# Top-32 pieces one step later, and the second expert layer's turning begun inside the attention's tail

## The chip, the cores and the metric

One core of a Trainium2 chip runs the whole kernel in one launch. The metric is the device time of an execution in microseconds; the time of a kernel is the median of its runs. Five engines work beside each other and meet through semaphores: TensorE (PE; PEld is its weight load), VectorE (DVE), ScalarE (ACT), GpSimd (POOL) and SyncE (SP), which issues most of the DMAs.

## The reference, cut to what matters

A decoder of two layers on `x` (2 x 512 tokens of 128) and a context (2 x 77 tokens of 128). Each layer adds three sublayers, each behind a layer norm. The second layer is where most of the change lies:

```python
# layer 1, behind layer 0 (attention, cross attention, experts that pick tokens)
x = x + L1_attn(layernorm(x))     # 16 heads of 64, causal softmax, then w_o
x = x + L1_xattn(layernorm(x))    # 16 heads of 8 on the 77 context tokens: scores, the 32
                                  # largest of a row, softmax over these, weighted values, Wo
x = x + L1_ffn(layernorm(x))      # 8 experts, the 2 best of a token:
#   h = relu(x @ Wg[e].T) * (x @ Wu[e].T); out_e = h @ Wd[e].T; sum of shares * out_e
```

## The kernel before

The tokens are worked in four blocks k of 256 (k = 0, 1 are batch 0, k = 2, 3 batch 1). The programs of the five engines are written out by hand, one loop for each engine over the same steps, and the order of each engine's instructions is the order of these loops.

**Attention of layer 1.** 48 steps U (`NU`), each one or two (head pair, query tile) units. At step U TensorE makes the scores of U + 2, turns the weights of U (`turn`, waiting for GpSimd's `divide(U)`) and sums values; VectorE finds row maxima (`row_max(U + 2)`) and reciprocal sums (`row_inv(U + 1)`), ScalarE copies the turned weights (`evac_pt(U)`) and makes the exponentials (`exps(U + 2)`), GpSimd divides (`divide(U + 1)`).

**Top-32 pieces.** The cross attention of layer 1 is cut into 16 pieces n of 4 heads x 256 tokens (4 pieces a block). A piece takes four quarters r on VectorE: in each eight MAX8 find the 8 largest of a row and eight MATCH_REPLACE8 remove them (`eight`, `remove`, lines 1207 and 1217). Around it: TensorE's `scores_x(n + 1)` and ScalarE's copy at r = 0, GpSimd's `shift(n)` at r = 1 and `gone(n - 1)`, `pick(n - 1)` (the mask and its product) at r = 0, ScalarE's exponential at r = 2, TensorE's transposes `weights_x(n - 1)` at r = 1 and 2 with ScalarE's copies `weights_T`, and `context(n - 1)` at r = 2. Pieces 0 to 9 run beside the attention, at steps that `piece_of(U)` names. Pieces 10 to 15 run behind it, at a late step `at` that `piece_late(at)` names (line 82): the helpers `cross`, `cross_one` and `cross_two` of each engine look it up.

**Late steps.** Three loops follow the attention, on every engine:
- b = 0 to 7, *the turning of the experts*. For each expert TensorE turns three 512-column parts of its weights (`turn_f(b, k)`, line 2473), ScalarE copies the first two as high parts (`w_hi`, line 1751) and the third as it is (`fd`), TensorE subtracts the high part (`minus_hi`), ScalarE copies the rest as low parts (`w_lo`, line 1755). Banks alternate over two experts. At b = 0 come route, the choice of two experts for batch 0's tokens and the last output projection; VectorE then works out the places of the tokens sorted by expert, GpSimd scatters the rows (line 800) and SP loads them back as 15 tiles of 128 sorted rows (`xs`, line 601). Before the steps b ≥ 2 end, `keep_busy` adds three matmuls without use (bank 7).
- j = 0 to 14 (`NS`), *the sorted tiles* of batch 0: `up_rows`, relu on ScalarE, `gate` on VectorE (line 1334), `hidden_T`, ScalarE's `evac_h`, `down_rows`. At j = 1, 5 and 9 `rows_T` turns the next four tiles into the same bank 7 that `hidden_T` uses.
- i = 0 to 31, *the dense half steps* of batch 1: all 8 experts for both blocks k = 2, 3, with `up`, `gate`, `down` and `combine`.

The late step is b, then 8 + j, then 23 + i. The norms, the context projection and the choice of experts for blocks 2 and 3 stand at fixed j and i behind the pieces that they need.

**What a wait for bank 4 means.** All late work of the top-32 pieces and of their norms goes through bank 4; `four` is the pair (semaphore, count) that says when ScalarE or VectorE has read what lies in it. In the same way `seven` guards bank 7.

```python
def piece_late(step):
    return divmod(40 + step, 4) if step <= 26 else (None, None)
```

Of the kernel before, what the change touches and what calls it, by code (L numbers as in the profile page):

```python
# [81 lines left out]
def piece_late(step):  # L82

    return divmod(40 + step, 4) if step <= 26 else (None, None)
# [26 lines left out]
def decoder(nc, x_in, ctx_in, a0_wq, a0_bq, a0_wk, a0_bk, a0_wv, a0_bv, x0_wq, x0_bq, x0_wk, x0_bk, x0_wv,  # L111
# [5 lines left out]
    with ExitStack() as held:  # L117
# [498 lines left out]
        def _(pool):  # L616
# [137 lines left out]
            for U in range(NU):  # L754
# [14 lines left out]
                if U + 1 < NU:  # L769
                    divide(U + 1)  # L770
# [58 lines left out]
            for j in range(NS):  # L829
                if j == 6:  # L830
                    rstd_two(2, gn_var, gn_rstd)
# [3 lines left out]
                if j == 9:  # L835
                    tokens_lo(2)
            for i in range(2 * E):
                if i == 7:
                    rstd_two(3, gn_var, gn_rstd)
                if i == 10:  # L840
# [7 lines left out]
        def _(dve):  # L848
# [401 lines left out]
            for U in range(NU):  # L1250
# [3 lines left out]
                if U + 1 < NU:  # L1254
# [160 lines left out]
            for j in range(NS):  # L1415
                gate(j)
                if j == 3:
                    context_norm(2)
                if j == 5:
                    add_context(2, ps[:, 4, 0:2 * P])  # L1420
                if j == 10:
                    gates(1, 4, 2, 4)
                if j == 12:
# [4 lines left out]
            for i in range(4 * E):  # L1428
# [3 lines left out]
                if i == 4:  # L1432
                    context_norm(3)
                if i == 6:
                    add_context(3, ps[:, 4, 0:2 * P])
                if i == 11:
                    gates(2, 6, 2, 4)
                if i == 13:
                    shares_of(2, 6, 2)
                if i == 14:  # L1440
# [8 lines left out]
        def _(act):  # L1449
# [232 lines left out]
            for U in range(NU):  # L1682
# [26 lines left out]
                evac_pt(U)  # L1709
                if U + 2 < NU:  # L1710
# [19 lines left out]
                if r == 1 and n >= 1:  # L1730
# [83 lines left out]
            for b in range(E):  # L1814
# [5 lines left out]
                cross_one(b)  # L1820
                for k in range(2):
# [8 lines left out]
                if b == 7:  # L1830
                    evac_xs(0)
            relu(0)
            for j in range(NS):
# [8 lines left out]
                if j == 3:  # L1842
                    evac_cn(2, four)
                if j == 6:
                    apply_two(2, gn_rstd, gn_ready)
                if j == 7:
                    norm_two(2, gnT_ps, gnT_ready, four)
                if j == 9:
                    tokens_hi(2)
                if j == 10:  # L1850
                    gates(1, 4, 2)
            for i in range(4 * E):
# [6 lines left out]
                if i == 4:  # L1859
                    evac_cn(3, four)  # L1860
                if i == 7:
                    apply_two(3, gn_rstd, gn_ready)
                if i == 8:
                    norm_two(3, gnT_ps, gnT_ready, four)
                if i == 9:
                    tokens_hi(3)
                if i == 11:
# [4 lines left out]
        def _(pe):  # L1872
# [158 lines left out]
            def values_x():  # L2031
                pe.wait_ge(qx_ready, 2)
                for b in range(B):
                    vo = ps[0:NC, 1, b * D:(b + 1) * D]
                    mm(vo, ctxT[:, b, :], w_x1T[:, 2, :], stop=False)
                    last = mm(vo, ones[0:1, 0:NC], bias_row("x1_bv"), start=False)
                last.then_inc(cross_ps, 1)
# [334 lines left out]

# [351 lines left out]
```

## Time and profile before

| | us |
|---|---|
| median of 3 runs | 583.12 |
| the runs | 580.05, 583.12, 586.41 |
| profiled execution | 580.95 |
| its span, first to last instruction | 579.2 |
| mean granted TensorE clock of it | 0.991 |

The span has these stages: layer 0 up to about 130 us, the attention of layer 1 up to 389.4, the turning of the experts up to 426.8, the sorted tiles up to 489.1, the dense half steps up to the end. Times in the rows below are microseconds from the span's start. A row of a timeline gives the start, the time from the first start to the last end, the engine, the line, the operation with what it writes and reads, and in brackets the idle time ahead of it with what ended it. Many instructions of TensorE have one line because one helper records them.

### The profile page before, as it was taken

Reading aid. Unit: us, or ns where it says so; the run is one execution under the profiler, and the core shown is the slowest. Engines: PE = TensorE matmul, PEld = TensorE weight load, DVE = VectorE, ACT = ScalarE, POOL = GpSimd, SP = SyncE. Lnnn points to the kernel's source line nnn. Section 1 sums busy time; section 2 is a strip of 40 time slices with the busy share of each in tenths; the row PEclk is TensorE's granted clock in tenths of the full one; section 3 lists DMA queues with packets and bytes.
Section 4 is the critical chain, followed back from the end, with each engine's and each line's share of the span. In section 5 each row is a group of like instructions: output and inputs, shape, how many; then the busy total and the mean of one; then the engine's idle time right before and its main releaser. Section 6 shows DMA issues by size and latency. Waiting matters only on the chain.

```text
span 579.2 us, 12144 instructions
## 1 busy us (share of the span) xinstructions
PE 515.3 (89%) x3947; PEld 409.7 (71%) x3947; DVE 385.4 (67%) x2194; ACT 311.1 (54%) x779; POOL 224.8 (39%) x236
## 2 busy tenths in 40 slices
PE   4888779998998999988999879978899899999997
PEld 2566348856667667767677657767767778999997
DVE  3576866543533697766598899968957979544533
ACT  2243324437785777665875667646765565323221
POOL 5014940013444474553564556552831343430000
PEclk9999999999999999998998999989999999999999
DMA  4700105604000000000000000004500000000000
GB/s 111 219 1 15 55 16 169 195 11 156 1 1 0 3 1 2 1 2 1 2 2 2 2 1 2 1 2 131 191 2 15 15 15 20 24 24 2 28 1 10
DMA packets 24089, 21.04 MB, mean 36 GB/s; under 512 B 2175, under 2 KB 18643, under 8 KB 24027
## 3 DMA queue, kind: packets, MB, share of 16 engines
q1 hardware_dynamic: 23515, 19.21, 11.0%
q0 software_dynamic: 512, 1.05, 0.6%
q8 instruction: 33, 0.54, 0.4%
q14 instruction: 29, 0.24, 0.1%
HBM read 17.22 MB, written 3.03 MB: 35 GB/s over the span
## 4 chain that ended last, share of the span: by engine, by line
PE 61%; DVE 15%; ACT 12%; issue 6%; POOL 5%; DMA 1%; DVEq 0%; ACTq 0%; POOLq 0%
PE ps L1874 51%; PE ps L2267 5%; ACT w_mem L1604 3%; DVE wk L1217 2%; PE ps L2329 2%; DVE sel_mem L1024 2%; ACT f_mem L1566 2%; DVE top L1207 1%; ACT pr L1604 1%; POOL xs_dram L800 1%; DVE nmax L1162 1%; PE ps L2541 1%; DVE bn L855 1%; POOL wk L743 1%; DVE xn L868 1%
## 5 line engine op out<-in xcount | busy, mean ns | idle before, releaser
L1162 DVE TENSOR_REDUCE nmax<-ps 128x2 f32<-128x256 f32 (+1 forms) x64 | 51.2, 821 | 59.6 <-PE ps L1874 57.5
L1217 DVE MATCH_REPLACE8 wk<-top,wk 128x77 f32<-128x77 f32 x384 | 80.6, 224 | 0.0
L712 POOL TENSOR_TENSOR w_mem<-w_mem,rinv 128x256 f32<-128x256 f32 (+3 forms) x44 | 53.1, 1218 | 50.9 <-DVE rinv L1168 50.4
L1334 DVE TENSOR_TENSOR sel_mem<-gr,ps 128x512 f32<-128x512 f32 x47 | 32.2, 686 | 48.3 <-ACT gr L1810 47.8
L1810 ACT ACTIVATE gr<-ps 128x512 f32<-128x512 f32 x47 | 28.1, 598 | 60.0 <-PE ps L1874 59.9
L1207 DVE MAX8 top<-wk 128x8 f32<-128x77 f32 x384 | 58.0, 224 | 0.2
L1874 PE MATMUL ps<-cat_mem 64*128 64x256 f32 (+7 forms) x276 | 56.8, 483 | 1.5 <-ACT cat_mem L1588 1.5
L1617 ACT ACTIVATE prT<-ps 128x768 f32<-128x768 f32 (+1 forms) x48 | 42.4, 883 | 21.3 <-PE ps L2267 20.8
L743 POOL TENSOR_SCALAR wk<-wk 128x616 f32<-128x616 f32 x16 | 28.1, 1754 | 53.7 <-DVEq L1221 53.4
L1604 ACT ACTIVATE w_mem<-ps,nmax 128x128 f32<-128x128 f32 (+3 forms) x88 | 44.5, 521 | 3.4 <-DVE nmax L1162 3.3
L1874 PE MATMUL ps<-prT,cat_mem 128*64 128x128 f32 x640 | 42.8, 281 | 3.3 <-DVE x L1242 1.8
L1874 PEld LDWEIGHTS ps<-prT,cat_mem 128*64 128x64 f32 x640 | 35.2, 139 | 9.6 <-issue 5.0
L712 POOL TENSOR_TENSOR pr<-pr,rinv 128x768 f32<-128x768 f32 (+3 forms) x20 | 26.6, 1341 | 28.0 <-DVE rinv L1168 27.6
L1874 PE MATMUL ps<-fd,sel_mem 128*128 128x128 f32 x256 | 34.5, 278 | 1.5 <-DVE sel_mem L1334 1.5
L1874 PE MATMUL ps<-x_hi,w_hi 128*128 128x256 f32 x128 | 34.6, 304 | 0.0
L1874 PEld LDWEIGHTS ps<-fd,sel_mem 128*128 128x128 f32 x256 | 31.2, 192 | 2.9 <-DVE sel_mem L1334 2.8
L1874 PE MATMUL ps<-later,ident 128*128 128x512 bf16 (+1 forms) x124 | 30.7, 369 | 1.8 <-ACT sel_mem L1665 0.7
L1874 PE MATMUL ps<-x_hi,w_lo 128*128 128x256 f32 x128 | 31.9, 282 | 0.0
L1588 ACT ACTIVATE cat_mem<-ps 128x512 f32<-128x512 f32 x32 | 19.4, 606 | 22.8 <-PE ps L1874 22.6
L2267 PE MATMUL ps<-ident,w_mem 128*128 128x128 f32 x212 | 30.5, 280 | 1.3 <-ACT cat_mem L1588 0.9
L1874 PEld LDWEIGHTS ps<-vh,sel_mem 77*128 77x128 f32 x256 | 29.8, 192 | 2.0 <-issue 0.9
L1217 DVE MATCH_VALUE_LOAD wk<-top,wk 128x8 f32 x384 | 30.9, 80 | 0.0
(362 smaller groups left out, 1313.9 us busy)
## 6 DMA issues: line engine op xcount, KB each, us to landing
w_mem<-in_L_ffn_W_dram SPq DMA_DIRECT2D x12, 256.0 KB, 3.2
f_mem<-in_L_ffn_Wg_dram SPq DMA_DIRECT2D x8, 256.0 KB, 2.9
f_mem<-in_L_ffn_Wu_dram SPq DMA_DIRECT2D x8, 256.0 KB, 3.7
f_mem<-in_L_ffn_Wd_dram SPq DMA_DIRECT2D x8, 256.0 KB, 4.2
sel_mem<-slot_dram SPq DMA_DIRECT2D x7, 256.0 KB
sel_mem<-in_L_ffn_W_dram SPq DMA_DIRECT2D x4, 256.0 KB, 4.0
xs_dram<-zero SPq DMA_DIRECT2D x1, 960.0 KB, 6.5
ys_dram<-f_mem SPq DMA_DIRECT2D x15, 64.0 KB, 1.5
```

Source lines behind the costliest of these rows:

```text
L712: pool.tensor_tensor(pr[s][:, :, at:at + n], pr[s][:, :, at:at + n], rinv[:, i % 8, :].unsqueeze(2).to_broadcast([P, 2, n]), ALU.mult)\
L743: pool.tensor_scalar(wk[q][:, :, :, :], wk[q][:, :, :, :], NEG, None, ALU.is_le)\
L1162: dve.tensor_reduce(nmax[:, i % 8, :], ps[:, 2 * s:2 * s + 2, at:at + (c + 1) * P], X, ALU.max, negate=True).then_inc(nmax_ready, 1)
L1207: dve.max(top[q][:, t, h, 8 * r:8 * r + 8], src[:, t, h, :]).then_inc(top_step, 1)
L1217: dve.match_replace(wk[q][:, t, h, :], top[q][:, t, h, 8 * r:8 * r + 8], src[:, t, h, :], GONE).then_inc(top_step, 1)
L1334: dve.tensor_tensor(hg[s][:, :], gr[s][:, :], ps[:, 2 * s + 1, :], ALU.mult)\
L1588: act.activation(qk_place(j), ps[:, bank, :].rearrange("p (w n) -> p w n", w=2), ACT.Copy)\
L1604: act.activation(pr[U % 3][:, h, at:at + (c + 1) * P], ps[:, 2 * s + h, at:at + (c + 1) * P], ACT.Exp, bias=nmax[:, i % 8, h:h + 1], accum ...
L1617: act.activation(prT[U % 3][:, :, 0:n], ps[:, 4:6, 0:n], ACT.Copy).then_inc(ptc_ready, 1)
L1810: act.activation(gr[j % 2][:, :], ps[:, 2 * (j % 2), :], ACT.Relu).then_inc(gr_ready, 1)
L1874: return pe.matmul(dst, lhsT, rhs, start=start, stop=stop, skip_group_check=shared)
L2267: last = pe.transpose(tiles(4 + h)[:, k, :], pr[U % 3][:, h, k * P:(k + 1) * P], ident[:, :])
```

## The change

- `piece_late` counts one step later: the late pieces begin at b = 1 instead of b = 0, and seven quarters instead of eight lie beside the turning. What followed a piece at a fixed j or i (context norm, its projection, norm, route and choice of block 2 and 3) moves by one step with it, but for the choice of block 2 at j = 14.
- Turning: two of the three parts of expert 0 (`turn_f(0, 0)`, `turn_f(0, 1)`, banks 0 and 1) move into step U = 45 of the attention. The three fillers of each b ≥ 2 go, the seven at the end become four and stand behind a wait for expert 6 only. The wait for the tile list and the loads of the first three tile numbers move from b = 1, 1, 2, 3 to b = 4, 4, 5, 6. At b = 7 `rows_T(0)` and ScalarE's `evac_xs(0)` stand ahead of the last corrections and low copies.
- Tail of the attention: ScalarE's first `weights_T(8)` stands ahead of the exponentials of U = 47; the reciprocals and the division of U = 47 stand ahead of `add_context(1)` and `rstd_two(1)`.
- Cross attention of layer 0: `values_x` is cut in two, and the halves stand ahead of and behind `weights_T0(1)`; the three fillers behind become six.

The diff, cut to its core:

```diff
 def piece_late(step):
-    return divmod(40 + step, 4) if step <= 26 else (None, None)
+    return divmod(39 + step, 4) if 1 <= step <= 27 else (None, None)
...
# GpSimd, attention
+                if U == NU - 2:
+                    divide(NU - 1)
                 for k in range(2):
                     if U == OUT[k] + 2:
                         rstd_two(k, gn_var, gn_rstd)
...
-                if U + 1 < NU:
+                if U + 1 < NU - 1:
                     divide(U + 1)
...
# VectorE, attention
-                if U + 1 < NU:
+                if U + 1 < NU - 1:
                     row_inv(U + 1)
...
+                if U == NU - 3:
+                    row_inv(NU - 1)
                 for k in range(2):
                     if U == OUT[k] + 1:
                         add_context(k, ps[:, 6, 0:2 * P])
...
# ScalarE, attention
                 evac_pt(U)
+                if U == NU - 3:
+                    weights_T(n - 1, 0, 7)
                 if U + 2 < NU:
                     exps(U + 2)
...
-                if r == 1 and n >= 1:
+                if r == 1 and n >= 1 and U != NU - 3:
                     weights_T(n - 1, 0, 7)
...
# ScalarE, turning
                 cross_one(b)
+                if b == 7:
+                    evac_xs(0)
                 for k in range(2):
                     evac_lo(b, k, F_BANKS[b % 2][k])
...
-                if b == 7:
-                    evac_xs(0)
...
# TensorE, layer 0
             context0(0)
+            values_x(0)
             weights_T0(1)
+            values_x(1)
             context0(1)
-            keep_busy(7, 3)
-            values_x()
+            keep_busy(7, 6)
...
# TensorE, attention (turn_f itself is only moved up)
                     if U == OUT[k] + 1:
                         project_context(k, six, (cat_ready, (26, 30)[k]))
+                        if U == NU - 3:
+                            turn_f(0, 0, (ex_ready, 2 * through(NU - 2)))
+                            turn_f(0, 1)
...
# TensorE, turning
+                    elif b == 0 and k < 2:
+                        continue
                     else:
                         turn_f(b, k)
...
-                if b >= 2:
-                    keep_busy(7, 3)
+                if b == 7:
+                    seven = rows_T(0, (place_step, 4))
                 for k in range(2):
                     minus_hi(b, k)
...
-                if b == 1:
+                if b == 4:
                     pe.wait_ge(place_step, 4)
-                if b in (1, 2, 3):
-                    experts.append(expert_of_tile(b - 1))
-                if b == 7:
-                    seven = rows_T(0, (place_step, 4))
+                if b in (4, 5, 6):
+                    experts.append(expert_of_tile(b - 4))
+            pe.wait_ge(w_lo_ready, 2 * E - 2)
+            keep_busy(0, 4)
             pe.wait_ge(fT_ready, 3 * E)
             pe.wait_ge(w_lo_ready, 2 * E)
-            keep_busy(0, 7)
             up_rows(0)
...
# sorted tiles and dense half steps, TensorE (as an example; the other engines likewise)
-                if j == 3:
+                if j == 4:
                     four = context_T(2, out_x, *four)
-                if j == 4:
+                if j == 5:
                     four = project_context(2, out_x, *four)
...
```

## Rows read from the trace of the kernel before

**Rows 1.** The page, its first line.
```profile
span 579.2 us, 12144 instructions
```

**Rows 2.** Four stretches: length, busy us of PE, PEld, DVE, ACT, POOL, PEclk, DMA.
```profile
372.00:389.40 17.40, 13.80 (x120) 11.07 (x121) 12.85 (x99) 8.34 (x18) 10.91 (x9) 0.90 0.01 2
389.40:426.80 37.40, 33.17 (x239) 27.76 (x239) 30.84 (x247) 27.44 (x58) 15.31 (x15) 1.00 0.41 126
426.80:489.10 62.30, 57.27 (x367) 47.66 (x368) 50.00 (x357) 33.41 (x74) 24.33 (x19) 1.00 0.05 14
489.10:579.20 90.10, 85.45 (x719) 83.50 (x717) 44.91 (x169) 25.57 (x49) 12.65 (x13) 1.00 0.05 15
```

**Rows 3.** The chain of waits, attention's tail: start, us, engine, what, line.
```profile
376.29 1.44 ACT pr L1604 x4
377.74 0.48 ACT sel_mem L1665
...
378.26 0.88 PE ps L2329 x4
```

**Rows 4.** Short stretches in the tail, columns as in rows 2.
```profile
376.50:377.00 0.50, 0.00 (x0) 0.00 (x0) 0.50 (x5) 0.50 (x3) 0.50 (x1) 1.00 0.04 16
...
380.00:381.00 1.00, 1.00 (x8) 0.67 (x9) 0.89 (x7) 0.55 (x1) 0.82 (x2) 0.50 0.00 0
```

**Rows 5.** Timeline of TensorE in the tail, the same matmuls twice.
```profile
368.94 1.75 PE L1874 MATMUL ps<-prT,cat_mem 128*64 128x128 f32 x28
...
380.35 2.53 PE L1874 MATMUL ps<-prT,cat_mem 128*64 128x128 f32 x28
```

**Rows 6.** Timeline of TensorE, turning and first sorted tile.
```profile
390.31 1.55 PE L2482 MATMUL ps<-ident,f_mem 128*128 128x128 f32 x12
...
401.68 1.54 PE L2482 MATMUL ps<-ident,f_mem 128*128 128x128 f32 x12 [1.86 <-issue]
...
412.48 0.81 PE L1874 MATMUL ps<-later,ident 128*128 128x512 bf16 x3
...
418.02 0.63 PE L2329 MATMUL ps<-ident,ex_mem 128*77 128x128 f32 x4 [0.93 <-POOL ex_mem L750]
...
426.84 1.67 PE L1874 MATMUL ps<-later,ident 128*128 128x512 bf16 x7 [0.60 <-ACT w_lo L1755]
...
428.16 0.58 PE L1874 MATMUL ps<-w_hi,xs_hi 128*128 x1
...
432.26 0.76 PE L1874 MATMUL ps<-kh,qc 128*128 128x308 f32 x2
```

**Rows 7.** Timeline of VectorE: last instruction of the tile list, two gates.
```profile
400.51 0.16 DVE L1368 TENSOR_SCALAR tile_id<-tile_e 1x15 int32<-1x15 f32 x1
...
430.66 0.69 DVE L1334 TENSOR_TENSOR sel_mem<-gr,ps 128x512 f32<-128x512 f32 x1 [5.91 <-ACT gr L1810]
...
434.05 0.68 DVE L1334 TENSOR_TENSOR sel_mem<-gr,ps 128x512 f32<-128x512 f32 x1
```

**Rows 8.** Timeline of ScalarE in the turning, high and low copies.
```profile
411.46 1.10 ACT L1751 ACTIVATE w_hi<-ps 128x512 fp32r<-128x512 f32 x2
...
413.68 1.08 ACT L1755 ACTIVATE w_lo<-ps 128x512 fp32r<-128x512 f32 x2
```

**Rows 9.** Timelines of GpSimd and SP: first row scatter, reloads of the sorted rows.
```profile
403.58 1.25 POOL L800 DMA_INDIRECT xs_dram<-xn,place_id  x1 [0.19 <-issue]
...
414.99 2.29 SPq L601 DMA_DIRECT2D xs<-xs_dram  x4
```

**Rows 10.** DMA issues, 380 to 440 us: count, KB each, median us to landing.
```profile
xs<-xs_dram SPq DMA_DIRECT2D x3, 256.0 KB, 4.0
```

**Rows 11.** TensorE's waits, 427 to 491 us: total us, times, longest us.
```profile
PE ps L2512 <- ACT f_mem L1772: 2.2, 3, 0.7
...
PE ps L1874 <- ACT sc L1644: 1.0, 2, 0.5
```

**Rows 12.** Timeline of TensorE in layer 0's cross attention.
```profile
46.62 0.66 PE L2048 MATMUL ps<-ident,cat_mem 128*77 128x128 f32 x4 [0.71 <-ACT cat_mem L1488]
```

More of the change, by code:

```diff
@@ L829, in _ @@
             for j in range(NS):
-                if j == 6:
+                if j == 7:
                     rstd_two(2, gn_var, gn_rstd)
@@ L1841, in _ @@
                 cross_two(E + j)
-                if j == 3:
+                if j == 4:
                     evac_cn(2, four)
-                if j == 6:
+                if j == 7:
                     apply_two(2, gn_rstd, gn_ready)
-                if j == 7:
+                if j == 8:
                     norm_two(2, gnT_ps, gnT_ready, four)
-                if j == 9:
+                if j == 10:
                     tokens_hi(2)
-                if j == 10:
+                if j == 11:
                     gates(1, 4, 2)
@@ L2029, in keys, with values_x @@
                 mm(ps[:, 0, 0:B * NC], w_x1T[:, 1, :], ctxT[:, :, :]).then_inc(cross_ps, 1)
-            def values_x():
+            def values_x(b):
                 pe.wait_ge(qx_ready, 2)
[L2033 to L2037, printed above, removed]
+                vo = ps[0:NC, 1, b * D:(b + 1) * D]
+                mm(vo, ctxT[:, b, :], w_x1T[:, 2, :], stop=False)
+                last = mm(vo, ones[0:1, 0:NC], bias_row("x1_bv"), start=False)
+                if b == B - 1:
+                    last.then_inc(cross_ps, 1)
             def scores_x0(b):
@@ L2371, in turn_two, with turn_f @@
                 return ((xnT_ready, 7 + k),)
+            def turn_f(m, k, *free):
+                for signal, count in free:
+                    pe.wait_ge(signal, count)
+                if k == 0:
+                    pe.wait_ge(in_f1[m % 4], 48 * (m // 4 + 1))
+                for c in range(FC):
+                    part_f = fn[m % 4][:, k, c, :]
+                    if k == 2:
+                        part_f = fn[m % 4][:, 2, :, :].rearrange("d a b -> d (a b)").rearrange("d (p c) -> d c p", c=FC)[:, c, :]
+                    last = pe.matmul(tiles(F_BANKS[m % 2][k])[:, c, :], part_f, ident[:, :], start=c == 0, stop=c == FC - 1,
+                                     is_transpose=True, skip_group_check=True)
+                last.then_inc(fT_ps, 1)
             pe.wait_ge(xin_ready, E)
@@ L2468, in _ @@
                         project_context(k, six, (cat_ready, (26, 30)[k]))
+                        if U == NU - 3:
+                            turn_f(0, 0, (ex_ready, 2 * through(NU - 2)))
+                            turn_f(0, 1)
                     if U == OUT[k] + 3:
                         norm_two(k, gn_ready, gnT_ps, gnT_ready, six, (v_ready, 15), (cat_ready, (27, 31)[k]))
-            def turn_f(m, k, *free):
-                for signal, count in free:
-                    pe.wait_ge(signal, count)
-                if k == 0:
-                    pe.wait_ge(in_f1[m % 4], 48 * (m // 4 + 1))
-                for c in range(FC):
-                    part_f = fn[m % 4][:, k, c, :]
-                    if k == 2:
-                        part_f = fn[m % 4][:, 2, :, :].rearrange("d a b -> d (a b)").rearrange("d (p c) -> d c p", c=FC)[:, c, :]
-                    last = pe.matmul(tiles(F_BANKS[m % 2][k])[:, c, :], part_f, ident[:, :], start=c == 0, stop=c == FC - 1,
-                                     is_transpose=True, skip_group_check=True)
-                last.then_inc(fT_ps, 1)
             def route(k, first, n, bank, *free):
```

46 lines of the change are left out of this document (23 added, 23 removed).

## The prediction

> **What bounds the kernel now.** I read the page first, then the stretches of the four stages that the change touches, then the chain of waits and the timelines of single engines inside them. The span is 579.2 us [rows 1], and 207 us of it lie in the stages from the attention's tail to the end [rows 2]. In none of the four is an engine full: TensorE is busy 13.8 of 17.4 us in the tail, 33.17 of 37.4 while the second expert layer's weights are turned, 57.27 of 62.3 over the 15 sorted row tiles (4.15 us a tile) and 85.45 of 90.1 over the 32 dense half steps (2.8 us a step). TensorE sets the pace with small waits on ScalarE, VectorE and GpSimd between its pieces, and part of its busy time in the turning is filler (`keep_busy`). So the question is which waits go, and which waits the fillers had been covering.
>
> **The attention's tail, U = 45 to 47.** At 376.29 ScalarE starts the exponentials of U = 47, 1.44 us, and only behind them the copy of turned weights (0.48) that TensorE needs for its next transposes at 378.26 [rows 3]. TensorE stood still, and in the stretch 380 to 381 the granted clock was 0.50, the 1.2 GHz level, after an idle 376.5 to 377 still listed at 1.00 [rows 4]. The same 28 matmuls that took 1.75 us at full clock took 2.53 there [rows 5]. After the change the copy stands ahead of the exponentials: ready at 376.29 + 0.5 = 376.8. TensorE fills the time with eight transposes of expert 0 and is back at the top-32 work by about 377.0, 1.3 us sooner. The exponentials then end at 378.2 (0.5 later), the copies behind them at 379.4, and the 28 matmuls run 379.5 to 381.2 at full clock instead of 380.35 to 382.88. That is 1.6 us; I take **1.5**, with 0 as the other end, if the new 1.3 us wait (378.1 to 379.4) still brings the low clock. Row_inv and divide of U = 47 change places with add_context and rstd_two: no instruction more, and what gets later (rstd by one divide) is needed only by norm_two(1), which waits for a ScalarE copy behind context(8) anyway. The new waits before turn_f(0, 0), for the exponentials of U = 46, were met before 376.29, since U = 47 comes after them on ScalarE [rows 3].
>
> **The turning of the eight experts.** What goes from TensorE's line: eight of the twelve transposes of expert 0, which took 1.55 together [rows 6], 1.0; the wait of 1.86 for the tile list at expert 1, whose last instruction on VectorE is at 400.51 [rows 7], because that wait now stands at expert 4; the wait of 0.93 on GpSimd's pick at 418.02, because the transposes that need it come one expert later; six fillers of three matmuls and three of the seven at the end. Seven fillers start at 426.84 and the next matmul at 428.16, 0.19 each [rows 6], so 21 of them are 4.0. Together 1.0 + 1.86 + 0.93 + 4.0 = 7.8.
>
> What comes back: each expert needs five ScalarE copies, two of 1.10 for the pair (high), two of 1.08 (low) [rows 8] and one between, some 2.6, and a piece's copies 0.5 or more [rows 3], 3.2 in all; TensorE without filler needs about 2.4: twelve transposes 1.55, two corrections of a filler's size 0.4, a piece's matmuls 0.4 or more [rows 6]. Over experts 4 to 7 TensorE therefore meets ScalarE and waits some 0.4 each, 1.6. At expert 2 the transposes of pick(9) now come right ahead of norm_two(3), both through bank 4, so norm_two waits for a copy that stands behind two low copies (1.08 and its own 0.5): 1.3. Queries(3) at expert 3 waits behind the copy of context(9), 0.4. Sum 3.3. **Net 7.8 − 3.3 = 4.5.** The ends: 7.8 if nothing comes back, and 1.0 + 1.86 + 0.93 − 1.3 = 2.5 if the fillers covered only waits. The stage's floor is ScalarE's work, 27.44 us [rows 2]; my 37.4 − 4.5 = 33 leaves it 83% busy.
>
> The three register loads of tile numbers move with the wait from experts 1 to 3 to 4 to 6: same number, priced at nothing because they cost the same there. No DMA changes its order on SP or POOL; the third load of the next weights still waits for expert 0's last four transposes. GpSimd's mask and pick of piece 9 move behind rstd_two(3); they fill an idle of GpSimd (15.31 us busy of 37.4 [rows 2]) ahead of the shift that precedes the row scatter, which itself waits for VectorE's first quarter; without that idle the scatter would start later by both. The scatter begins at 403.58, SP's reloads are issued at 414.99 [rows 9] and land within 4.0 [rows 10], 419.0. The chain to it hangs on add_attention(3), which comes 1.5 + 1.0 sooner, so 416.5. Rows_T(0) now stands ahead of the last corrections, and evac_xs(0) ahead of the last two low copies: whoever waits there holds up the stage's end. I put TensorE there at about 417.7, a cover of 1 us; without it the end would wait as long as the data is late.
>
> **The clock rule, weighed.** Rows: the clock fell to 0.50 after TensorE's idle at 376.5 [rows 4], yet after the 1.86 wait at 401.68 [rows 6] the stage still shows 1.00 [rows 2]. The Trainium skill (TensorE: Matmul & The Clock Gate, "What's actually happening") says that the array is throttled by default and that recent activity lifts the throttle; by it every filler taken out is a risk. By that rule the sum would lose some or all of its gain; by the row of the turning stage it loses nothing. I follow the row and keep the rule as a rival.
>
> **The sorted tiles and the dense steps.** Of TensorE's waits there, three of 0.7 (2.2 us) stand before rows_T, on the copy of the hidden tile, and two of 0.5 on the copy of scores [rows 11]. One step later the first scores matmul of a piece (two take 0.76 [rows 6], so 0.4) falls exactly into the three steps with rows_T: 3 × 0.4 = 1.2. At step 0 the second scores matmul waited with nothing between; now down_rows stands between: 0.5. Together 1.7. Against it VectorE: quarter 3 of piece 11, which ran ahead of gate(0) in an idle of 5.91, now runs behind it, and the last quarter falls to dense step 1. A gate with a quarter takes 434.05 − 430.66 = 3.39 [rows 7], a dense step 2.8, so up to 0.6; the context matmuls one step earlier give slack, so 0.2. **Net 1.5**, ends 1.7 and −0.6.
>
> **Edits at nothing.** values_x in two halves goes into waits of 0.71 at 46.62 [rows 12] and the one after it; VectorE's context additions are behind them either way. Six fillers for three there end before the next norm. Without that cover: 0.3.
>
> **Sum.** 1.5 + 4.5 + 1.5 = 7.5 us. The span 579.2 becomes 571.7, the profiled execution 580.95 becomes 573.4. The median of the runs shown, 583.12, lies 2.2 above that execution and the three runs spread over 6.4; carried over to the median: 583.1 − 7.5, rounded, **575.5**.
>
> **Rivals.**
> 1. The fillers only covered waits on ScalarE (the turning yields 2.5, the tail 1.0): 3.5, with 0 to 1 from the tiles: 579.2. For it: ScalarE was busy 27.44 of 37.4 us, and the copies come in bursts. Against: the three fillers at 412.48 have no wait ahead of them [rows 6].
> 2. VectorE becomes the bound of the sorted tiles, because one quarter more (2.8) lies behind gate(0): 1.5 + 4.5 − 2.8 = 3.2, 579.9. For it: 3.39 a tile for a gate and a quarter, 50.0 of 62.3 busy. Against: TensorE's mean of 4.15 a tile.
> 3. A low clock once or twice, as at 380, in the tail or the turning: about 1.7 each (the 28 matmuls of the tail alone lost 0.78, the transposes ahead of them and the ones behind as much again [rows 5]); 577 to 579. It needs a TensorE idle like that at 376.5; the new waits of 1.3 are shorter.
> 4. Slower: with the fillers gone the clock stays at the 1.2 GHz level from expert 2 to 7. Some 20 us of TensorE's 33.17 there would take twice as long, less 5 of waits that it fills: 15 us more, 590.5. It decides from the point where half rate costs more than the 7.5 gained, about 13 us of TensorE work. For it: the drop at 380. Against: 1.00 in the stage with a 1.86 wait in it.
>
> **How the numbers follow.** Forecast 0.55, its own range 572.5 to 578.5; rival 1 0.20, rival 2 0.09, rival 3 0.09, rival 4 0.07. The terms' ends sum to 1.6 + 7.8 + 1.7 = 11.1 and 0 + 2.5 − 0.6 = 1.9, which is 572.0 to 581.2 from the median; with its spread 570 to 581.5, which leaves out rival 4 and a tenth for the ends. One per cent, 5.8 us, is about what a measurement can tell from no change. Below 577.3 lie nine tenths of the forecast and a sixth of rivals 1 to 3: 0.56; above 589 only rival 4 and rounding, 0.07; the rest, 0.37, within.
>
> **What would show it.** The tail: route at about 387.9 instead of 389.4, and no row of PEclk below 1.00 between 378 and 382. The turning: up_rows(0) at about 422.2, six fewer fillers, no wait at expert 1, waits on ScalarE's low copies at experts 4 to 7, ScalarE at 80% or more. The tiles: rows_T waits of 0.3 instead of 0.7. I am wrong if waits on ScalarE in the turning exceed 5 us, if rows_T(0) waits for DMA, if PEclk shows 0.50 there, or if TensorE waits on gates.

## The result, and the profile after

Over 20 runs of each the changed kernel takes 580.12 us in the median and the kernel before 583.96. The ratio is 0.993, 95% interval 0.9907 to 0.9954: 4.1 us off, with 2.7 to 5.4 as the ends. Here and below the medians are over all runs, and the ratios leave out runs more than 1.5% above the fastest of their kernel (6 of the 20 of the kernel before, at 590.4 to 590.9 us, none of the changed kernel; below, 8 of the 12 of c1, one of them at 2764, and two of the 6 of a4, at 980 and 2097), so the two need not agree. The forecast was 7.5 us less, 575.5, with 572.5 to 578.5 as its range. The profiled execution takes 578.94 us.

The page of the changed kernel, its first line:

```profile
span 577.1 us, 12108 instructions
```

The same four stretches as in [rows 2], cut at the changed kernel's own borders:

```profile
372.00:388.20 16.20, 13.40 (x130) 10.51 (x128) 14.46 (x106) 8.98 (x22) 8.66 (x7) 1.00 0.01 2
388.20:423.90 35.70, 32.00 (x217) 26.46 (x218) 29.86 (x223) 27.84 (x59) 19.79 (x18) 0.95 0.42 132
423.90:485.50 61.60, 56.71 (x371) 47.94 (x369) 51.58 (x366) 33.36 (x73) 23.08 (x18) 1.00 0.05 15
485.50:577.10 91.60, 84.61 (x710) 82.40 (x709) 45.92 (x184) 25.29 (x48) 12.65 (x13) 1.00 0.05 15
```

The borders are round figures, so the stages are measured between instructions of TensorE that every kernel has: 28 matmuls of an earlier step of the attention, the route (8 matmuls of 128x8), the first `up_rows(0)`, the transposes of `hidden_T(14)`, and the end. Timeline of TensorE in the kernel before, the marks that [rows 6] lacks:

```profile
358.43 1.75 PE L1874 MATMUL ps<-prT,cat_mem 128*64 128x128 f32 x28
...
389.42 1.03 PE L1874 MATMUL ps<-wrT,xnT 128*128 128x8 f32 x8 [0.53 <-issue]
...
490.83 0.63 PE L2541 MATMUL ps<-ident,sel_mem 128*128 128x128 f32 x4
```

The same marks in the changed kernel:

```profile
359.36 1.75 PE L1880 MATMUL ps<-prT,cat_mem 128*64 128x128 f32 x28
...
388.24 1.03 PE L1880 MATMUL ps<-wrT,xnT 128*128 128x8 f32 x8 [0.53 <-issue]
...
423.92 0.58 PE L1880 MATMUL ps<-w_hi,xs_hi 128*128 x1
...
485.74 0.63 PE L2551 MATMUL ps<-ident,sel_mem 128*128 128x128 f32 x4
```

Differences of the marks give the stages, in us:

| stage | before | after | difference | forecast |
|---|---|---|---|---|
| tail (28 matmuls to route) | 30.99 | 28.88 | −2.11 | −1.5 |
| turning (route to up_rows(0)) | 38.74 | 35.68 | −3.06 | −4.5 |
| sorted tiles (to hidden_T(14)) | 62.67 | 61.82 | −0.85 | −1.7 |
| dense half steps (to the end) | 88.37 | 91.36 | +2.99 | +0.2 |
| sum | | | −3.03 | −7.5 |

The first mark is 0.93 us later in the changed kernel's execution, so its span is only 2.1 us shorter. The stage that went the wrong way is the last one, which the forecast had all but left alone.

**Where the dense steps lost 3 us.** TensorE's waits from `hidden_T(14)` to the end, changed kernel (total us, times, longest):

```profile
PE ps L1880 <- DVE sel_mem L1338: 3.1, 6, 1.1
PE ps L1880 <- ACT f_mem L1784: 0.9, 1, 0.9
```

and the kernel before:

```profile
PE ps L1874 <- DVE sel_mem L1334: 1.5, 4, 0.5
PE ps L2351 <- DVE sel_mem L1233: 0.2, 1, 0.2
```

Three of the waits stand at the first steps. Timeline of TensorE, changed kernel:

```profile
491.39 1.13 PE L1880 MATMUL ps<-fd,sel_mem 128*128 128x128 f32 x8 [0.94 <-ACT f_mem L1784]
...
496.35 1.16 PE L1880 MATMUL ps<-fd,sel_mem 128*128 128x128 f32 x8 [0.62 <-DVE sel_mem L1338]
...
500.06 1.16 PE L1880 MATMUL ps<-fd,sel_mem 128*128 128x128 f32 x8 [1.12 <-DVE sel_mem L1338]
```

VectorE's gate (L1338) is only the last link. It was itself idle for ScalarE's relu:

```profile
495.60 0.69 DVE L1338 TENSOR_TENSOR sel_mem<-gr,ps 128x512 f32<-128x512 f32 x1 [2.38 <-ACT gr L1816]
```

The chain starts on ScalarE, whose timeline there is:

```profile
490.49 0.59 ACT L1669 ACTIVATE sel_mem<-ps 77x512 f32<-77x512 f32 x1 [2.16 <-PE ps L2336]
490.99 0.26 ACT L1784 ACTIVATE f_mem<-ps 128x128 f32<-128x128 f32 x1
494.25 0.23 ACT L1663 ACTIVATE sel_mem<-ps 128x72 f32<-128x72 f32 x1 [3.00 <-PE ps L1880]
494.37 0.71 ACT L1656 ACTIVATE ex_mem<-ex_mem 128x616 f32<-128x616 f32 x1
494.98 0.59 ACT L1816 ACTIVATE gr<-ps 128x512 f32<-128x512 f32 x1
495.77 0.60 ACT L1816 ACTIVATE gr<-ps 128x512 f32<-128x512 f32 x1 [0.20 <-PE ps L1880]
```

ScalarE was idle 2.16 us for the second transposes of a piece and 3.00 us for its context; `evac_y(14)` (L1784) and the relu of a dense step (L1816, twice in a row because the first is late) stood behind them. They could have run in these waits. In the kernel before, whose pieces stand one step earlier, TensorE has no wait longer than 0.5 there.

**Where the turning fell short.** TensorE's timeline in the changed kernel, its waits and one low-clock group:

```profile
399.36 0.99 PE L1880 MATMUL ps<-w_hi,neg_ident 128*128 128x512 f32 x2 [0.41 <-ACT w_hi L1757]
...
401.77 0.44 PE L2310 MATMUL ps<-ident,xn 128*128 128x128 f32 x2 [0.98 <-ACT sel_mem L1669]
...
404.88 1.93 PE L1880 MATMUL ps<-vh,sel_mem 77*128 77x9 f32 x16 [0.40 <-ACT sel_mem L1669]
...
407.12 0.70 PE L1880 MATMUL ps<-xnT,w_x1T 128*128 128x256 f32 x2 [0.32 <-ACT sel_mem L1663]
407.66 2.59 PE L2389 MATMUL ps<-ident,f_mem 128*128 128x128 f32 x12
...
417.82 0.63 PE L2336 MATMUL ps<-ident,ex_mem 128*77 128x128 f32 x4 [1.01 <-POOL ex_mem L750]
```

Twelve transposes of expert 4 took 2.59 us instead of the 1.54 of an equal group in [rows 6], and the wait on GpSimd's pick is there as before. VectorE's and GpSimd's timelines show why the pick is no sooner. VectorE, list of places:

```profile
396.02 1.11 DVE L1354 TENSOR_TENSOR cum<-cum 128x8 f32<-128x8 f32 x3
...
398.11 1.47 DVE L1364 TENSOR_SCALAR place_id<-ends 128x4 int32<-128x4 f32 x1
```

GpSimd, the mask and product of piece 9, and the first row scatter:

```profile
396.21 1.76 POOL L743 TENSOR_SCALAR wk<-wk 128x616 f32<-128x616 f32 x1
398.05 1.50 POOL L750 TENSOR_TENSOR ex_mem<-ex_mem,wk 128x616 f32<-128x616 f32 x1
...
403.40 1.25 POOL L802 DMA_INDIRECT xs_dram<-xn,place_id  x1 [0.20 <-issue]
```

A tiny VectorE instruction that ends at 399.58 lies exactly under a GpSimd product that ends at 399.55. The scatter begins 0.18 us sooner than at 403.58 [rows 9], though `add_attention(3)`, the addition that its chain hangs on, comes 2.0 us sooner (393.52 against 395.55).

### The profile page after: what moved, and what is told of

It reads as the page before. It is cut to its first block, busy times and chain, and to the rows that moved or that the text cites. A ratio compares the mean times of both kernels' runs of the same rounds, so it can differ in the third digit from the quotient of the medians.

```text
span 577.1 us, 12108 instructions
## 1 busy us (share of the span) xinstructions
PE 513.5 (89%) x3929; PEld 408.6 (71%) x3929; DVE 387.7 (67%) x2194; ACT 311.0 (54%) x779; POOL 224.8 (39%) x236
## 3 DMA queue, kind: packets, MB, share of 16 engines
HBM read 17.22 MB, written 3.03 MB: 35 GB/s over the span
## 4 chain that ended last, share of the span: by engine, by line
PE 58%; DVE 19%; ACT 11%; issue 5%; POOL 5%; DMA 1%; DVEq 0%; ACTq 0%; POOLq 0%
PE ps L1880 48%; PE ps L2274 5%; DVE wk L1219 3%; ACT w_mem L1608 3%; DVE top L1209 2%; DVE sel_mem L1026 2%; PE ps L2336 2%; ACT f_mem L1570 2%; DVE sel_mem L1338 1%; DVE nmax L1164 1%; POOL xs_dram L802 1%; POOL wk L743 1%; ACT pr L1608 1%; PE ps L2551 1%; DVE bn L857 1%
## 5 line engine op out<-in xcount | busy, mean ns | idle before, releaser
L1338 DVE TENSOR_TENSOR sel_mem<-gr,ps 128x512 f32<-128x512 f32 x47 | 32.2, 686 | 47.6 <-ACT gr L1816 46.9
L1816 ACT ACTIVATE gr<-ps 128x512 f32<-128x512 f32 x47 | 28.1, 598 | 57.3 <-PE ps L1880 57.3
L1880 PE MATMUL ps<-cat_mem 64*128 64x256 f32 (+7 forms) x276 | 55.5, 473 | 1.5 <-ACT cat_mem L1592 1.5
L1880 PEld LDWEIGHTS ps<-prT,cat_mem 128*64 128x64 f32 x640 | 34.4, 136 | 10.2 <-issue 4.7
L1880 PE MATMUL ps<-vh,sel_mem 77*128 77x9 f32 x256 | 30.6, 256 | 0.4 <-ACT sel_mem L1669 0.4
```

The source lines that it names most:

```text
L1338: dve.tensor_tensor(hg[s][:, :], gr[s][:, :], ps[:, 2 * s + 1, :], ALU.mult)\
L1816: act.activation(gr[j % 2][:, :], ps[:, 2 * (j % 2), :], ACT.Relu).then_inc(gr_ready, 1)
L1880: return pe.matmul(dst, lhsT, rhs, start=start, stop=stop, skip_group_check=shared)
```

## The experiments

Stage times of all kernels, measured between the same marks, and the median of the runs with its ratio to the kernel before, run beside it:

| kernel | tail | turning | tiles | dense | median | ratio, 95% interval |
|---|---|---|---|---|---|---|
| before | 30.99 | 38.74 | 62.67 | 88.37 | 583.96 | |
| after | 28.88 | 35.68 | 61.82 | 91.36 | 580.12 | 0.993 (0.9907 to 0.9954) |
| a1_no_shift | 28.88 | 39.27 | 62.51 | 88.38 | 580.81 | 0.9938 (0.9901 to 0.9975) |
| a2_shift_only | 30.99 | 44.76 | 62.13 | 91.37 | 593.25 | 1.0187 (1.0118 to 1.0257) |
| a3_pool_early | 28.88 | 35.23 | 61.73 | 91.33 | 578.41 | 0.9917 (0.988 to 0.9955) |
| a4_relu_ahead | 28.87 | 35.68 | 61.75 | 87.41 | 577.35 | 0.9891 (0.9822 to 0.9961) |
| b1_both | 28.87 | 35.05 | 61.78 | 87.42 | 573.36 | 0.9809 (0.9765 to 0.9854) |
| b2_two_fillers | 30.16 | 33.89 | 61.81 | 87.35 | 573.34 | 0.979 (0.975 to 0.9831) |
| d1_quarter_first | 28.87 | 35.21 | 60.49 | 87.39 | 574.01 | 0.9808 (0.976 to 0.9857) |
| c1_before_pool_late | 32.50 | 46.40 | 62.59 | 88.36 | 593.2 | 1.0007 (0.9948 to 1.0067) |
| e1_evac_only | 28.87 | 35.67 | 61.76 | 90.50 | 578.89 | 0.9903 (0.9867 to 0.9939) |
| e0_after | 28.88 | 35.65 | 61.81 | 92.18 | 579.88 | 0.9924 (0.9894 to 0.9953) |
| d2_all | 28.87 | 34.60 | 60.42 | 87.33 | 572.49 | 0.9816 (0.976 to 0.9872) |
| d3_in_waits | 28.87 | 33.83 | 60.55 | 87.37 | 571.31 | 0.9825 (0.9784 to 0.9866) |

A stage whose instructions are in the same order repeats within 0.2 us from kernel to kernel wherever the clock falls at the same places (35.23, 35.21 and 35.05 for the turning of a3, d1 and b1); the runs as a whole spread by several us. So a mechanism is read from the stages, and the medians only say whether the whole moved.

### The shift of the pieces, taken out and alone

`a1_no_shift` is the changed kernel with `piece_late` and the steps that follow it as before; `a2_shift_only` is the kernel before with nothing but that.

```diff
# a1_no_shift, against the changed kernel (a2_shift_only: the reverse, against the kernel before)
-    return divmod(39 + step, 4) if 1 <= step <= 27 else (None, None)
+    return divmod(40 + step, 4) if step <= 26 else (None, None)
...
-                if j == 7:
+                if j == 6:
                     rstd_two(2, gn_var, gn_rstd)
...
```

> The changed kernel with the top-32 pieces left at their old steps; everything else of the change is in. Theory (the shift by one step costs 2 to 3 us in the dense steps, gains 0.9 in the sorted tiles, and hides one wait on GpSimd's pick in the turning): about 4.5 us under the kernel before, 0.991 to 0.994, so near the changed kernel. In the trace the first dense steps have no wait over 0.5 us, and the turning has a wait of 2 to 3 us on GpSimd's pick at expert 5. Rival (the shift is what the gain comes from): at most 2 us under the kernel before, 0.997 or more.

> The kernel before with the pieces one step later and nothing else. Theory: the dense steps lose 2 to 3 us, the sorted tiles gain 0.9, the turning gains 0.9 and loses what VectorE's list of places loses beside GpSimd's mask: together 1 to 3 us slower, 1.002 to 1.005. Rival (the shift is worth its gain by itself): 1 to 3 us faster, 0.995 to 0.998.

The dense steps settle one question: with the shift 91.36 and 91.37, without it 88.37 and 88.38. The shift alone costs these 3.0 us, whatever is done in the turning. In the sorted tiles it saves 0.54 (before to a2) or 0.69 (a1 to after).

In the turning the profiles list +0.5 us for the fillers and moves without the shift (a1), +6.0 for the shift without them (a2) and −3.1 for both together. The +0.5 is not the price of a1's order alone. Its profiled execution is the longest of its twelve (584.03 us, the shortest 576.96), and its transposes ran at the low clock twice in the turning, at experts 3 and 7, against once in the changed kernel. TensorE's timeline of a1 at expert 7:

```profile
425.34 2.80 PE L2389 MATMUL ps<-ident,f_mem 128*128 128x128 f32 x12
```

Against the 1.52 of such a group at full clock this second fall costs some 1.3 us, more than the 0.5. So whether a1's edits pay in the turning without the shift stays open. By stages a1 lies 1.7 us under the kernel before, not the 4.5 expected, and the wait of 2 to 3 us on the pick that was expected is 0.86.

TensorE's timeline of a2 shows what the shift does alone:

```profile
398.75 0.79 PE L1874 MATMUL ps<-kh,qc 128*128 128x308 f32 x2 [0.31 <-ACT sc L1644]
403.53 2.79 PE L2482 MATMUL ps<-ident,f_mem 128*128 128x128 f32 x12 [4.00 <-issue]
```

The wait for the tile list at expert 1, 1.86 in [rows 6], grows to 4.00. Some 0.3 of this is that the piece's transposes, which had stood ahead of the wait, now stand behind it. The rest is that the list comes later: its last instruction on VectorE starts at 402.26 instead of 400.51 [rows 7], with the route within 0.1 us of where it was. GpSimd's mask and product of piece 9 now run beside the list, and its additions and second place_id take 1.11 and 1.46 us as in the changed kernel, where TensorE asks for the list only at expert 4, long after it is done. The transposes after the wait run at half the clock. The stretch behind the wait, columns as in [rows 2]:

```profile
403.00:409.00 6.00, 5.47 (x21) 4.46 (x21) 5.79 (x49) 2.72 (x5) 4.29 (x4) 0.50 0.27 88
```

a2 was expected at 1.002 to 1.005 and came at 1.0187: neither this growth of the wait nor the clock behind it was foreseen. The longer wait is 2.1 of the 6.0; the rest goes with the groups at the low clock, there and once more at 416.79, where twelve transposes took 2.67 us.

### GpSimd's mask and product beside VectorE's list

`a3_pool_early` puts the mask and product of piece 9 ahead of everything in the turning, into GpSimd's idle time, instead of behind `rstd_two(3)`. `c1_before_pool_late` does the opposite to the kernel before.

```diff
# a3_pool_early, GpSimd
+            gone(9)
+            pick(9)
             for b in range(E):
                 if b == 1:
                     rstd_two(3, qn_var, qn_rstd)
-                cross(b)
+                if b != 1:
+                    cross(b)
# c1_before_pool_late, GpSimd, against the kernel before
                 if b == 1:
                     rstd_two(3, qn_var, qn_rstd)
-                cross(b)
+                    gone(9)
+                    pick(9)
+                if b:
+                    cross(b)
```

> The changed kernel with GpSimd's mask and pick of piece 9 back ahead of the loop over the experts, as before the change, where GpSimd idles. Theory (the two engines exclude each other on shared memory ports): VectorE's second place_id instruction falls from 1.47 us to 0.16 and the three cum additions from 1.11 to 0.57; the row scatter begins 1.5 to 1.9 us sooner after add_attention(3); TensorE's 1.0 us wait on the pick at expert 6 goes; 1.0 to 1.9 us under the changed kernel, 0.990 to 0.992 of the kernel before. Rival (VectorE was slow there for another reason, such as the DMAs of the weights): place_id stays over 1 us and the time within 0.3 us of the changed kernel.

> The kernel before with one order changed: GpSimd's mask and product of piece 9 behind rstd_two(3), so that they run beside VectorE's list of places. If these two engines get in each other's way there, the second place_id instruction takes 1.2 us or more instead of 0.16 and the three additions of cum over 1.0 instead of 0.57, the tile list comes 1 to 2 us later and TensorE's wait for it at expert 1 grows from 1.86 to 3 to 4 us: ratio 1.001 to 1.006. If something else of the change made them long, they stay at 0.16 and 0.57 and the time is that of before.

VectorE in a3, the same two groups:

```profile
394.29 0.57 DVE L1357 TENSOR_TENSOR cum<-cum 128x8 f32<-128x8 f32 x3
...
395.84 0.16 DVE L1367 TENSOR_SCALAR place_id<-ends 128x4 int32<-128x4 f32 x1
```

VectorE in c1:

```profile
407.06 1.11 DVE L1353 TENSOR_TENSOR cum<-cum 128x8 f32<-128x8 f32 x3
...
409.15 1.46 DVE L1363 TENSOR_SCALAR place_id<-ends 128x4 int32<-128x4 f32 x1
```

With nothing else changed, the one order makes the second place_id 1.46 us and the additions 1.11; the other order gives 0.16 and 0.57. That is shown in both directions. The Trainium skill (SBUF — State Buffer, "Who interferes with whom") says that VectorE's two-port modes, and its instructions with two inputs in SBUF beside a GpSimd instruction that reads SBUF, contend with GpSimd for one shared pair of ports, and that against a two-port mode the one that issues first keeps the pair for its whole instruction while the other is blocked. The place_id, which starts 0.06 us behind the product and ends 0.03 us behind it, agrees; that it ran in such a mode is not shown. The three additions of the changed kernel were slowed by 0.54 us, not held to the end of the mask at 397.97.

In a3 the scatter starts (399.83) 13.32 us behind route instead of 15.16, and the 1.01 us wait on pick is gone; a new one of 0.45 stands at expert 5. The stage takes 35.23, 0.45 less than after and less than half of the 1.0 to 1.9 expected. In c1 TensorE waits 2.35 us for the product and 1.18 for the list, 3.53 together where 1.86 stood. What c1's order costs the whole stays open: its median of 593.2 and its ratio of 1.0007 (0.9948 to 1.0067) point different ways, and its profiled execution had fallen to the low clock ahead of route (32.50 in the tail), so that its turning of 46.40 is not the order's price.

### ScalarE's order in the dense steps

`a4_relu_ahead` puts `evac_y(14)` ahead of the piece's copies at half step 0, and the relu of the next half step ahead of the piece's second copies. `e1_evac_only` moves `evac_y(14)` alone.

```diff
# a4_relu_ahead, ScalarE, dense half step i
-                if i:
-                    relu(NS + i)
+                if i == 0:
+                    evac_y(NS - 1)
                 cross_one(E + NS + i)
-                if i == 0:
-                    evac_y(NS - 1)
+                if i + 1 < 4 * E:
+                    relu(NS + i + 1)
                 cross_two(E + NS + i)
```

> The changed kernel with ScalarE's relu of dense step i + 1 ahead of the second half of step i's piece copies, and the copy of the last sorted tile's result ahead of the first half. Theory (the dense steps lost 2.7 us because relu and that copy stand on ScalarE behind copies that wait for TensorE's piece matmuls): the waits of 0.94, 0.62 and 1.12 us at the first dense steps fall under 0.3 each, 2 to 3 us under the changed kernel, 0.987 to 0.990 of the kernel before. Rival (the last quarters on VectorE are too much work there, whatever the order on ScalarE): the gate waits stay, under 0.7 us gained.

> The changed kernel with one order mended: at dense half step 0 ScalarE's evac_y(14) ahead of the piece's copies, the relus left where they are. If the two late copies are separate costs, only the wait of 0.94 us before the first dense down-projection goes and the two waits on gates of 0.62 and 1.12 us behind it stay: dense half steps 90.2 to 90.6 us instead of 91.4, ratio 0.990 to 0.994. If evac_y alone held everything up, all three waits go: 87.4 us, ratio 0.986 to 0.989.

TensorE's waits in the dense steps of a4:

```profile
PE ps L1880 <- DVE sel_mem L1338: 1.2, 3, 0.5
```

91.36 becomes 87.41, 3.95 us less, more than the 2 to 3 expected, and 0.96 less than in the kernel before. Of it 0.86 is `evac_y` (90.50 in e1, where the wait of 0.94 is gone and those of 0.62 and 1.12 stand as they were), and 3.1 the relus. At the first steps one wait on a gate is left, of 0.39. The cause of the loss is the order of the ScalarE queue behind the shift. The 0.96 beyond the loss may be worth having without the shift too; the order was not tried in the kernel before.

`b1_both` joins a3's and a4's edits.

> The changed kernel with both orders mended: GpSimd's mask and product of piece 9 ahead of rstd_two(3), and ScalarE's relu of the next dense half step ahead of the piece's second copies, evac_y(14) ahead of everything of step 0. If the two losses are separate places, the stages add up: route to up_rows(0) 35.2 us (as with the first edit alone), the dense half steps 87.4 us (as with the second alone), together some 4.4 us less than the changed kernel, span near 572, ratio to the kernel before 0.985 to 0.990. If they share a cause, only one of the two shows.

Its stages are those of the two parts within 0.2 us, 35.05 and 87.42, and its ratio of 0.9809 lies below what was expected.

### VectorE's last quarter of piece 11

In the changed kernel VectorE is idle ahead of `gate(0)` and late behind it. Timelines of VectorE and of TensorE there:

```profile
426.30 0.69 DVE L1338 TENSOR_TENSOR sel_mem<-gr,ps 128x512 f32<-128x512 f32 x1 [4.56 <-ACT gr L1816]
```

```profile
430.85 0.63 PE L2551 MATMUL ps<-ident,sel_mem 128*128 128x128 f32 x4 [1.18 <-DVE sel_mem L1338]
```

`d1_quarter_first` is b1 with that quarter ahead of the gate.

```diff
# d1_quarter_first, VectorE
             for j in range(NS):
+                if j == 0:
+                    cross(E)
                 gate(j)
...
-                cross(E + j)
+                if j:
+                    cross(E + j)
```

> Both orders mended, and on VectorE the last quarter of piece 11 ahead of gate(0), in the idle time of 4.6 us that stands there. If VectorE's quarter behind gate(0) is what makes TensorE wait on gates (rival 2 in a small form), the wait of 1.2 us before the second sorted tile's transposes goes and the waits on gates from up_rows(0) to the first dense step fall from 2.6 us to 1.5 or less, the stage from 61.8 to 60.3 to 61.0 us. If the pace is TensorE's own, the stage stays at 61.5 to 62 us.

TensorE's waits on the gate from `up_rows(0)` to `hidden_T(14)` were 2.6 us in the changed kernel, three of them, the longest 1.2. In d1:

```profile
PE ps L2557 <- DVE sel_mem L1341: 1.4, 2, 0.8
```

The stage falls from 61.78 to 60.49, 1.3 us. The medians of the runs do not resolve it (574.01 against 573.36).

### The clock at expert 4

Each of the seven kernels after, e0, e1, a3, a4, b1 and d1, which share TensorE's order in the turning and have no filler at experts 2 to 6, lists 2.33 to 2.66 us for expert 4's twelve transposes. `b2_two_fillers` is b1 with three fillers back at experts 2 and 3; `d2_all` has these and d1's edit; `d3_in_waits` replaces the six by nine that stand inside the waits listed above.

```diff
# b2_two_fillers, d2_all: TensorE, turning, ahead of minus_hi
+                elif b in (2, 3):
+                    if b == 2:
+                        pe.wait_ge(place_step, 4)
+                    keep_busy(7, 3)
# d3_in_waits: TensorE, turning
+                if b == 3:
+                    keep_busy(7, 2)
                 four = cross_two(b, *four)
                 if b == 2:
+                    pe.wait_ge(place_step, 4)
+                    keep_busy(7, 5)
                     four = norm_two(3, qn_ready, qnT_ps, qnT_ready, out_x, *four)
                 if b == 3:
+                    keep_busy(7, 2)
                     four = queries(3, out_x, *four)
```

> The last one with three fillers put back at experts 2 and 3 (the wait for the tile list stands ahead of the first). If the fall of the clock at expert 4 comes from the fillers that were taken out, the granted clock of the turning is 1.00 and expert 4's twelve transposes take 1.5 us instead of 2.6, for 1.1 us of fillers that partly fill waits: the stage 34.0 to 34.9 us. If the waits on ScalarE ahead of norm_two(3) bring the fall, it stays below 0.97 and the stage takes 35.3 to 36.3 us.

> All four edits together: both orders mended, three fillers at experts 2 and 3, VectorE's last quarter of piece 11 ahead of gate(0). If the gains add up by stage: turning 33.9 us at granted clock 1.00, sorted tiles 60.5, dense 87.4, tail 18.4 from the landmark matmuls of U = 44; about 2.3 us less than with the two orders alone, ratio to the kernel before 0.975 to 0.982. If a saving in one stage is given back in the next (quarter first makes the turning's end later, or the clock falls elsewhere), the ratio is that of the two orders alone, 0.981 to 0.985.

> The changed kernel as it is, beside the other two on one chip: 0.991 to 0.995 of the kernel before, turning 35.2 to 36.2 us, sorted tiles 61.8, dense half steps 91.4.

> The kernel with all four edits, its six fillers replaced by nine that stand inside the waits of the turning: five ahead of norm_two(3) at expert 2 (wait 0.99 us), two ahead of context(9) and two ahead of queries(3) at expert 3 (0.39 and 0.32). At 0.19 us each they cost next to nothing. If the fall of the clock at expert 4 comes from TensorE standing still in these waits, expert 4's twelve transposes take 1.5 us, the granted clock of the turning is 1.00 and the stage takes 33.4 to 34.2 us. If it comes whatever fills them (as once with the six fillers ahead of the corrections), the transposes take 2.5 us or more and the stage 34.6 to 35.4 us.

Timeline of TensorE at expert 4 in b2:

```profile
408.93 1.52 PE L2392 MATMUL ps<-ident,f_mem 128*128 128x128 f32 x12
```

in d2:

```profile
407.48 2.74 PE L2395 MATMUL ps<-ident,f_mem 128*128 128x128 f32 x12
```

and in d3, with the fillers in the largest wait (400.13) and two of the others:

```profile
400.13 1.24 PE L1886 MATMUL ps<-later,ident 128*128 128x512 bf16 x5
...
403.82 0.61 PE L1886 MATMUL ps<-later,ident 128*128 128x512 bf16 x2
...
406.16 0.59 PE L1886 MATMUL ps<-later,ident 128*128 128x512 bf16 x2
407.16 1.52 PE L2395 MATMUL ps<-ident,f_mem 128*128 128x128 f32 x12
```

The turning of d3, columns as in [rows 2]:

```profile
387.75:421.58 33.83, 32.39 (x227) 25.89 (x227) 30.51 (x243) 27.41 (x59) 19.17 (x18) 1.00 0.43 139
```

With six fillers ahead of the corrections the granted clock stayed at 2.4 GHz through expert 4 once and fell once (33.89 and 34.60 us for the stage); with nine inside the waits it stayed, 33.83. These are one profiled execution each, and b2's clock had fallen ahead of the route just before (30.16 in the tail), so that waits on ScalarE rather than the lack of fillers as such bring the fall is supported, not proven. d2 missed its expected 33.9 by this, and kept the rest (60.42, 87.33). e0 repeats the changed kernel; its dense steps took 0.8 us longer because the clock fell there too, behind the wait of 0.94.

d3 has the smallest sum of stages, 10.2 us less than before and 7.1 less than after, and the lowest median: 571.31 us against 584.13 for the kernel before on its chip, ratio 0.9825, 0.9784 to 0.9866. The ratios of b1, b2, d1, d2 and d3, 0.979 to 0.9825, do not tell these five apart.

## Why the prediction was wrong, point by point

**The sum.** The forecast of −7.5 stands against −3.03 by stages. The terms that missed are dense +2.8, turning +1.4, tiles +0.85; the tail gave 0.6 more. Another 0.8 lies in the level: the forecast started from 583.12, the median of three runs, and 20 runs put the kernel before at 583.96.

**Tail: right, sized too low.** TensorE, changed kernel:

```profile
376.99 1.04 PE L2389 MATMUL ps<-ident,f_mem 128*128 128x128 f32 x8
377.86 0.66 PE L2336 MATMUL ps<-ident,ex_mem 128*77 128x128 f32 x4
378.36 0.84 PE L2274 MATMUL ps<-ident,w_mem 128*128 128x128 f32 x6
379.94 1.75 PE L1880 MATMUL ps<-prT,cat_mem 128*64 128x128 f32 x28 [0.74 <-DVE x L1244]
```

The 28 matmuls take 1.75 instead of 2.53 [rows 5], with no low clock between them and the route. They start at 379.94; without the 0.93 by which this execution is late that is 379.0, 1.34 sooner than before, where the forecast had 379.5. The two gains, 1.34 and 0.78, are the 2.11 of the stage. The new wait was put at 1.3 and is 0.74, on VectorE and not on ScalarE's copies. The edits do not keep the low clock away for good: in b2, which has them, it fell ahead of the route and the tail took 30.16.

**Turning: one term left out, one row read wrongly.** The step that failed first is that GpSimd's mask and pick of piece 9 only "fill an idle of GpSimd". It looked only at GpSimd's own queue. The 3.3 us of work do fit there, but they lie beside VectorE's list of places and stretch it, and the wait of 0.93 on pick, counted as gone, stayed at 1.01; mending the order gives 0.45 to 0.6 back (a3, b1). Second, the clock: the row that decided for "it loses nothing" (1.00 with a wait of 1.86 in the stage) was measured with the fillers in the stage that the change takes out. It could not speak for the stage without them. The price of the fall is some 1.4 us (35.21 in d1, 33.83 in d3). Rival 3 named this mechanism and held that it needs an idle like that at 376.5; here the clock fell behind waits of 0.98, 0.40 and 0.32. The Trainium skill's rule (TensorE: Matmul & The Clock Gate, "What's actually happening") that the array is throttled by default and activity lifts the throttle was the better guide here. The traces agree in part: expert 4's group took 2.59 us without fillers and 1.52 with nine inside the waits, but with six ahead of the corrections once 1.52 and once 2.74. Rival 4, the clock low from expert 2 to 7, did not come; the loss was one group and its neighbours. With the order and the waits mended the stage takes 33.83 us, 4.9 less than before, so the 4.5 were there to be had. The wait ahead of `norm_two(3)`, forecast at 1.3, is 0.98; the waits on low copies at experts 4 to 7, forecast at 1.6, do not appear in the changed kernel.

**The parts were not separate terms.** The sum priced the shift and the turning's moves one by one. a2 shows that the shift alone costs 6.0 in the turning, falls of the clock included: it stretches VectorE's list of places, and the wait for that list has to move from expert 1 to 4 before the shift can pay. What the moves give without the shift is not known (a1's +0.5 includes a second fall of the clock).

**Sorted tiles: rival 2, at a fraction.** The waits ahead of rows_T went from 2.2 [rows 11] to 0.2 and those for scores from 1.0 to 0.5, as forecast; but waits on gates rose from 0.6 to 2.6. The forecast saw that quarter 3 of piece 11 "now runs behind" gate(0) and charged 0.2 for it at the far end of the chain. Its price is 1.3 (d1), paid at the second tile.

**Dense steps: the step that failed most, 2.8 of the 4.5 us by which the stages miss.** The text asked what one step later does to VectorE's last quarter, and answered 0.2. It never walked ScalarE's program there: relu and `evac_y` behind copies that wait for TensorE's transposes and context. The shift costs 3.0 us there (a1, a2), and a4's order gives back 3.95. None of the rivals named it; rival 1's time of 579.2 lies near the result by luck: it puts the miss into the turning and the tail, which gave more than it says (3.06 and 2.11 against 2.5 and 1.0), and nothing into the dense steps.

**values_x at nothing: no difference shown.** The first mark, which lies behind these edits, stands between 357.48 (b1) and 363.16 (a1) in the kernels that have them and between 358.35 (a2) and 363.25 (c1) in those that do not; single executions differ there by more than the 0.3 at stake.

## What to carry to other kernels

When a chain of work is moved by one step, walk every engine's program at its new place to the end of the kernel and ask of each instruction behind a wait whether somebody now hangs on it; an instruction that is ready belongs ahead of the one that waits. Before taking out fillers, list the waits that remain without them: those are the ones to fill, as far as one profile (d3) shows, rather than the stretches in which TensorE is busy anyway. And an idle slot on GpSimd is free only if VectorE's small instructions beside it are not on the path.

## What the hardware showed that was not expected

A VectorE instruction on 128x4 elements took 0.16 us alone and 1.46 and 1.47 beside a GpSimd product of 128x616; three additions of 128x8 took 0.57 and 1.11.

TensorE's granted clock fell to its 1.2 GHz level behind a wait of 4.00 us (a2), and at expert 4 behind waits of 0.98, 0.40 and 0.32 us; in the kernel before, with the fillers in place, a wait of 1.86 had left it at 2.4 GHz. The falls come at places that can differ from one execution to the next (at expert 4 in d2 and not in b2, whose orders there are the same; ahead of the route in b2 and c1; at experts 3 and 7 in a1), and go with the spread between runs of one kernel: an execution of a1 with a mean clock of 0.991 took 577.3 us, one with 0.979 581.1.
